# Degrees and scaling of a graph layer: zeros in quarters, a short reciprocal, low parts on VectorE

## The chip, the cores and the metric

The kernel runs on 1 core of one Trainium2 chip. Its time is device microseconds of one execution; the figure for a kernel is the median of its runs.

## The reference

1250 nodes with 512 features each, 21,250 weighted edges (1250 of them loops), ten propagation steps, then an LSTM over the 1250 rows in which each step picks one of four weight sets:

```python
def _L0_gnn_ref(x, alpha, beta, sigma, edge_val, edge_row, edge_col, num_iters):
    xn = x * rsqrt(maximum(sum(x * x, axis=1, keepdims=True), 1e-12))
    sim_e = sum(xn[edge_row] * xn[edge_col], axis=-1)
    sim_e = where(edge_row == edge_col, 0.0, sim_e)
    sim_e = exp(sim_e / (2.0 * sigma_sq))            # sigma_sq = 2 exp(sigma)^2
    sup = edge_val * sim_e
    normalize = segment_sum(sup, edge_row, num_segments=n)
    denom = b + normalize[:, None] * a + a           # a = exp(alpha), b = exp(beta)
    def step(out, _):
        Ax = segment_sum(sup[:, None] * out[edge_col], edge_row, num_segments=n)
        return (x * b + (Ax + out) * a) / denom, None
    out, _ = scan(step, x, None, length=10)

x = x + _L0_gnn_ref(_layernorm(x), alpha, beta, sigma, edge_weight, src, dst, 10)
x = x + _L0_ffn_ref(_layernorm(x)[None], ...)[0]     # the LSTM with a choice of weight set per step
```

## The kernel before

The graph is worked as a dense matrix. The 1250 nodes are padded to NP = 1280, ten row blocks (RT) of 128 partitions. The steps follow each other in this order.

**Head.** VectorE (from line 619) zeroes the last block of X, then all 12,801 columns of the SBUF tile Adj1 (line 620), then sets `ones` and `ident` and zeroes the three edge tiles; the last of these (`ew`, line 625) releases six edge loads on ScalarE's DMA queue (lines 492 to 495), which already carries five small loads. SyncE's queue loads X (lines 286, 287) and then, released by the zeros, writes Adj1 into each of two adjacency tensors in DRAM (lines 289 to 291, 51,204 bytes to a partition). TensorE spreads the scalars over the partitions when `ones` and the five small loads are there (line 908), VectorE copies them out (631), ScalarE, whose program has the six edge issues first, forms exp(alpha), exp(beta) and exp(-2 sigma) (498, 499), and VectorE scales the last (633). Only behind this wait does VectorE do the layernorm and the normalization (661 to 670). TensorE transposes the result, ScalarE takes it out of PSUM (513).

**Scatter.** 42 rounds of four edge columns: VectorE writes the keys on a diagonal (691), TensorE spreads them over the partitions by a product with `ones` (941), VectorE compares (694, 695), TensorE sums the weights of edges with equal keys (944), and GpSimd scatters them into the DRAM tensors by an indirect DMA (371 to 379, profile line 375) with a wait for an earlier one to have landed. The first scatter waits for the zeros (366). Between the rounds TensorE computes the similarities and ScalarE their exponentials into Adj.

**Adjacency.** SyncE's queue reads the two tensors back, row block by row block (293 to 300). VectorE adds them in Adj1 (720) and multiplies the sum into Adj (723).

**Degrees.** When all ten blocks are done, TensorE sums Adj over its rows, column piece by column piece (512, 512, 256), all row blocks of a piece one after the other; because the left operand is `ones`, each degree stands in every partition (951 to 955). An f32 matmul has two records in the profile. VectorE then forms 1/(a deg + b + a) for all 1280 columns in every partition (726 to 729) into inv_b, takes its diagonal blocks as per-partition columns `den` (730 to 732), and scales (733 to 735).

**Scaling and splitting.** For each row block, VectorE multiplies Adj by inv_b (738) and adds the diagonal (740); ScalarE rounds the block to f16, the high part (526); GpSimd subtracts it from the f32 value, which gives the f16 low part (411, 412). Both go into M_parts, which lies over Adj1. VectorE waits for all ten low parts (743), writes T (745) over Adj, and ScalarE and GpSimd split T in the same manner (530, 416).

**Propagation** (lines 750 to 755, 957 to 971) is ten times 300 f16 matmuls of 128x512. **After it** come the residual, a second layernorm, the projections of the first 64 rows and the splitting of the recurrent weights. **Recurrence** (lines 829 to 886, 1000 to 1082): each of the 1250 steps computes the gates with a guessed weight set and, where the guess was wrong, again with the chosen one (`repeated`). Fifteen semaphores are raised by one by VectorE ahead of it (824 to 826); the first logit product waits for `c_ready`, the fourteenth of them.

The order is set by each engine's program order and the semaphores. Where `link` stands, VectorE waits for its own instruction's end before the next.

Of the kernel before, what the change touches and what calls it, by code (L numbers as in the profile page):

```python
# [5 lines left out]
def gnn_then_selected_lstm(  # L6
# [40 lines left out]
    ITERS = 10  # L47
    COLS = [(c, min(512, NP - c)) for c in range(0, NP, 512)]
# [21 lines left out]
    with ctx:  # L70
# [66 lines left out]
        inv_b = sim[:, 0, :]  # L137

# [76 lines left out]
        deg_mm = sem("deg_mm")  # L215
        prop_mm = sem("prop_mm")
# [66 lines left out]
        def _(sp):  # L283
# [6 lines left out]
            for b in range(2):  # L290
                sp.dma_start(adj[b].rearrange("(p n) -> p n", p=P), Adj1[:, :]).then_inc(adj_zeroed, 16)
# [61 lines left out]
        def _(pool):  # L353
# [9 lines left out]

            last_word = pool.alloc_register("last_word")
            pool.reg_mov(last_word, P * CW - 1)
            pool.wait_ge(adj_zeroed, 32)
# [42 lines left out]

            for r in range(RT):  # L410
                pool.wait_ge(m_high, r + 1)
                pool.tensor_tensor(M_parts[:, 1, r, :], Adj[:, r, :], M_parts[:, 0, r, :], ALU.subtract).then_inc(m_low, 1)
# [198 lines left out]
        def _(dve):  # L611
# [8 lines left out]
            dve.memset(Adj1[:, :], 0.0).then_inc(zero_set, 1)  # L620
# [4 lines left out]
            dve.memset(ew[:, :], 0.0).then_inc(edge_ready, 1)  # L625
            for s in range(S):
                link(dve.memset(ramp[:, s:s + 1], float(S - s)))
# [97 lines left out]
            dve.wait_ge(deg_mm, 1)  # L725
            for c, (c0, m) in enumerate(COLS):
                link(dve.tensor_scalar(inv_b[:, c0:c0 + m], ps[:, c, 0:m], ab[:, 0:1], ab[:, 1:2], ALU.mult, ALU.add))
            link(dve.tensor_scalar(inv_b, inv_b, ab[:, 0:1], None, ALU.add))
            link(dve.reciprocal(inv_b, inv_b))
            for r in range(RT):  # L730
                link(dve.scalar_tensor_tensor(out=junk[:, 0, :], in0=inv_b[:, r * P:(r + 1) * P], scalar=1.0, in1=ident[:, :],
                                              op0=ALU.mult, op1=ALU.mult, accum_out=den[:, r:r + 1]))
            link(dve.tensor_scalar(adn[:, :], den[:, :], ab[:, 0:1], float(2 ** MS), ALU.mult, ALU.mult))
            link(dve.tensor_scalar(bdn[:, :], den[:, :], ab[:, 1:2], float(2 ** OS), ALU.mult, ALU.mult))
# [169 lines left out]
        def _(pe):  # L904
# [47 lines left out]
            for c, (c0, m) in enumerate(COLS):  # L952
                for r in range(RT):
                    last = nc.tensor.matmul(ps[:, c, 0:m], ones[:, :], Adj[:, r, c0:c0 + m], start=(r == 0), stop=(r == RT - 1))
# [192 lines left out]
```

## Time and profile before

| | |
|---|---|
| median of 3 runs | 6814.86 us (6814.09 to 6822.49) |
| profiled execution, its own time | 6817.24 us |
| its span, first to last instruction | 6815.5 us |
| mean granted TensorE clock | 0.959 |
| busy: PE matmul, VectorE, ScalarE, GpSimd | 6117.3, 3616.7, 1805.4, 1686.4 us |
| DMA moved | 389.94 MB |

All times below are microseconds from the span's start unless marked ns. PE is TensorE's matmul, PEld its weight load, DVE VectorE, ACT ScalarE, POOL GpSimd, SP SyncE; ACTq and SPq are their DMA queues. A timeline row has its start, its duration, the engine, the line, the operation, output and inputs by name and shape, xN where N such instructions are merged, and in brackets how long the engine was idle before it and what ended that. Tiles that lie over one another appear under one name: Adj in a row can be Adj1, T or M_parts, and sim can be inv_b. A source-line row has the count, minimum, median and maximum duration in ns and the first and last start. On the page a group has busy time and mean ns of one, then the idle time before it and its releaser. The clock is the share of full speed that was granted.

### The profile page before, as it was taken

Reading aid. Unit: us, or ns where it says so; the run is one execution under the profiler, and the core shown is the slowest. Engines: PE = TensorE matmul, PEld = TensorE weight load, DVE = VectorE, ACT = ScalarE, POOL = GpSimd, SP = SyncE. Lnnn points to the kernel's source line nnn. Section 1 sums busy time; section 2 is a strip of 40 time slices with the busy share of each in tenths; the row PEclk is TensorE's granted clock in tenths of the full one; section 3 lists DMA queues with packets and bytes.
Section 4 is the critical chain, followed back from the end, with each engine's and each line's share of the span. In section 5 each row is a group of like instructions: output and inputs, shape, how many; then the busy total and the mean of one; then the engine's idle time right before and its main releaser. Section 6 shows DMA issues by size and latency. Waiting matters only on the chain.

```text
span 6815.5 us, 340711 instructions
## 1 busy us (share of the span) xinstructions
PE 6117.3 (90%) x126674; PEld 4119.5 (60%) x126675; DVE 3616.7 (53%) x19152; ACT 1805.4 (26%) x6561; POOL 1686.4 (25%) x4128
## 2 busy tenths in 40 slices
PE   6727999789999999999999999999999999999986
PEld 3523444666666666666666666666666666666663
DVE  5553111245565556555665555566556655556555
ACT  1001000522332223223332333233333333233321
POOL 4733111412222222222222222222222222222220
PEclk8758999589999999999999999999999999999999
DMA  3230000622222122122222222222222222222210
GB/s 95 1 77 0 0 0 0 192 71 58 62 63 58 57 60 65 55 60 60 65 63 60 62 61 60 60 63 63 61 60 65 64 61 63 59 63 62 61 52 27
DMA packets 691011, 389.94 MB, mean 57 GB/s; under 512 B 47835, under 2 KB 670811, under 8 KB 690720
## 3 DMA queue, kind: packets, MB, share of 16 engines
q1 hardware_dynamic: 659746, 369.66, 18.5%
q0 software_dynamic: 24192, 0.10, 1.1%
q10 hardware_dynamic: 7038, 19.69, 0.9%
q8 instruction: 26, 0.43, 0.0%
q14 instruction: 9, 0.07, 0.0%
HBM read 370.96 MB, written 18.38 MB: 57 GB/s over the span
## 4 chain that ended last, share of the span: by engine, by line
PE 70%; DVE 6%; issue 5%; DMA 1%; DVEq 0%; SPq 0%; ACT 0%; POOL 0%; POOLq 0%
PE ps L1016 33%; PE ps L1078 15%; PE ps L1025 8%; PE ps L1009 5%; PE ps L1005 4%; DVE hsum L843 2%; PE ps L1002 2%; PE ps L991 1%; DVE osum L851 1%; DVE acts L861 1%; DVE gates L848 1%; DVE osum L854 1%; DMA wring<-in_w_ih 1%; DVE cprod L857 0%; PE ps L978 0%
## 5 line engine op out<-in xcount | busy, mean ns | idle before, releaser
L1016 PE MATMUL ps<-WH,hparts 128*2 128x384 f16 x49760 | 2303.0, 326 | 196.6 <-issue 176.1
L1016 PEld LDWEIGHTS ps<-WH,hparts 128*2 128x2 f16 x49760 | 1053.4, 83 | 1044.7 <-issue 292.9
L843 DVE TRANSPOSE_TENSOR_REDUCE hsum<-ps 128x12 f32<-128x384 f32 x1250 | 728.7, 583 | 1793.0 <-PE ps L1016 1788.0
L1078 PE MATMUL ps<-xcur,wcur 128*128 128x64 f32 x9728 | 1341.9, 281 | 85.7 <-issue 12.4
L1078 PEld LDWEIGHTS ps<-xcur,wcur 128*128 128x128 f32 x9728 | 1178.5, 191 | 273.3 <-issue 210.2
L454 POOL COPY xT<-hfull 128x4 f32 x1250 | 239.5, 192 | 3727.2 <-DVE hfull L872 3727.2
L470 POOL COPY wcur<-wring 128x512 f32<-128x512 f32 x1216 | 743.4, 611 | 445.1 <-ACT gxb L598 443.3
L1025 PEld LDWEIGHTS ps<-WH,hparts 128*2 128x2 f16 x40000 | 603.7, 83 | 352.7 <-issue 314.9
L1025 PE MATMUL ps<-WH,hparts 128*2 128x128 f16 x40000 | 781.2, 219 | 7.5
L583 ACT ACTIVATE gx_now<-gxb 128x16 f32 x1250 | 269.7, 216 | 1782.2 <-DVE pick L837 1707.1
L969 PE MATMUL ps<-O,Adj 128*128 128x512 f16 x3000 | 650.3, 380 | 77.2 <-DVEq L748 77.2
L598 ACT ACTIVATE gxb<-ps,ubias,gscale 128x64 f32 x1216 | 562.2, 462 | 327.4 <-PE ps L1078 247.5
L586 ACT ACTIVATE acts<-gates 128x12 f32<-128x12 f32 x1250 | 265.4, 212 | 1378.1 <-DVE gates L848 1378.1
L969 PEld LDWEIGHTS ps<-O,Adj 128*128 128x128 f16 x3000 | 294.1, 98 | 433.3 <-issue 81.1
L1005 PE MATMUL ps<-wselT,acts 128*1 128x4 f32 x10000 | 433.4, 166 | 20.4 <-DVE acts L861 4.2
L1009 PE MATMUL ps<-owsel,tanc 128*1 128x4 f32 x10000 | 428.1, 166 | 0.0
L851 DVE TRANSPOSE_TENSOR_REDUCE osum<-ps 128x4 f32<-128x128 f32 x1250 | 385.4, 308 | 0.1
L754 DVE SCALAR_TENSOR_TENSOR Adj<-ps,Adj 128x512 f32<-128x512 f32 x100 | 69.2, 692 | 582.2 <-PE ps L969 582.2
L1005 PEld LDWEIGHTS ps<-wselT,acts 128*1 128x1 f32 x10000 | 317.6, 81 | 54.2 <-DVE acts L861 48.1
L1009 PEld LDWEIGHTS ps<-owsel,tanc 128*1 128x1 f32 x10000 | 326.8, 81 | 31.2
L588 ACT ACTIVATE otan<-osum 128x4 f32<-128x4 f32 x1250 | 256.6, 205 | 263.8 <-DVE osum L854 263.8
L375 POOL DMA_INDIRECT adjacency<-total,where_ x168 | 261.4, 1556 | 129.4 <-issue 79.4
(147 smaller groups left out, 4983.8 us busy)
## 6 DMA issues: line engine op xcount, KB each, us to landing
wring<-in_w_ih SPq DMA_DIRECT2D x1280, 256.0 KB, 2.9
gxb<-in_w_hh ACTq DMA_DIRECT2D x32, 512.0 KB, 5.6
adjacency<-Adj SPq DMA_DIRECT2D x2, 6400.5 KB, 24.7
Adj<-adjacency SPq DMA_DIRECT2D x10, 640.0 KB, 7.5
sim<-adjacency SPq DMA_DIRECT2D x10, 640.0 KB, 6.3
adjacency<-total,where_ POOLq DMA_INDIRECT x168
x_rows<-X SPq DMA_DIRECT2D x1, 2560.0 KB, 8.7
wring<-x_rows SPq DMA_DIRECT2D x10, 256.0 KB, 3.5
```

Of the source, the lines that this page charges most:

```text
L470: pool.tensor_copy(wcur[:, :, :], wring[:, u, :, :]).then_inc(wcur_set, 1)
L583: act.activation(gx_now[:, :], gxb[:, bass.ds(t % (2 * TB), 1), bass.ds(r * (G * SUB) - G * SUB, G * SUB)].rearrange("p t c -> p (t c)"), ...
L586: act.activation(acts[:, 0:3 * SUB], gates[:, :], ACT.Tanh, scale=1.0 / GATE_SCALE).then_inc(acts_ready, 1)
L598: act.activation(gxb[:, bass.ds(((b + 1) % 2) * TB, TB), bass.ds(i, 1)].rearrange("p t c -> p (t c)"), unit_ps, ACT.Identity, scale=gscale ...
L843: dve.tensor_reduce(hsum[:, :], gate_ps.rearrange("p (c q) -> p c q", q=32), AX.X, ALU.add, apply_transpose=True).then_inc(turned, 1)
L851: dve.tensor_reduce(osum[:, 0, :], ogate_ps.rearrange("p (c q) -> p c q", q=32), AX.X, ALU.add, apply_transpose=True).then_inc(oturned, 1)
L969: last = nc.tensor.matmul(ps[:, r % 8, :], M_parts[:, m_part, c, r * P:(r + 1) * P], old[:, o_part, c, :], start=(c == 0 and m_part + o_pa ...
L1005: nc.tensor.matmul(logit_ps, acts[:, 3 * SUB + k:3 * SUB + k + 1], wselT[:, k, :], start=False, stop=False)
L1009: last = nc.tensor.matmul(logit_ps, tanc[:, k:k + 1], owsel[:, k, :], start=False, stop=(k == SUB - 1))
L1016: last = nc.tensor.matmul(gate_ps[32 * j:32 * j + 2, :], hparts[:, k, :], WH[:, s * KC + k, part, j, 0:3 * P], start=(k == 0 and part == 0 ...
L1025: last = nc.tensor.matmul(ogate_ps[32 * j:32 * j + 2, :], hparts[:, k, :], WH[:, s * KC + k, part, j, 3 * P:4 * P], start=(k == 0 and part ...
L1078: last = nc.tensor.matmul(unit_ps, wcur[:, k, :], xcur[:, k, :], start=(k == 0), stop=(k == KC - 1))
```

## The change

The zeros: Adj1's first quarter (ZC = 3201 columns) alone is zeroed, after the memset of the edge weights, and each adjacency tensor is zeroed by four DMAs from it. The degrees: the loops change places, so that TensorE sums a row block as soon as it is masked, into three PSUM banks. The reciprocal: VectorE takes the ten per-partition degrees from the diagonals of the sums, forms the reciprocal of these 10 columns alone, writes a (1/den) 2^15 on ten diagonal 128x128 tiles, TensorE spreads each over the partitions by a product with `ones`, and VectorE copies the result to inv_b in three pieces. The low parts of the matrix go from GpSimd to VectorE, each behind the next block's product. Five of the fifteen counts ahead of the recurrence are raised by GpSimd before its first scatter.

```diff
--- before.py
+++ after.py
@@ -45,6 +45,8 @@
     NN = NP * NP
     CW = NN // P + 1
     ITERS = 10
+    ZC = -(-CW // 4)
+    ZEROS = [(z, min(ZC, CW - z)) for z in range(0, CW, ZC)]
     COLS = [(c, min(512, NP - c)) for c in range(0, NP, 512)]
     TB = 64
     BLOCKS = -(-N // TB)
@@ -135,6 +137,7 @@
         XB = adj_words[:, 0:RT * D].rearrange("p (t d) -> p t d", t=RT)
         T = adj_words[:, RT * D:2 * RT * D].rearrange("p (t d) -> p t d", t=RT)
         inv_b = sim[:, 0, :]
+        adiag = [one[:, q, :] for one, part in ((kdiag, range(NQ)), (same, range(NQ)), (junk, range(2, NQ))) for q in part]
 
 
         WH = sb("WH", [P, S * KC, 2, 4, D], f16)
@@ -213,6 +216,8 @@
         sim_exp = sem("sim_exp")
         adj_ready = sem("adj_ready")
         deg_mm = sem("deg_mm")
+        adiag_set = sem("adiag_set")
+        arow_mm = sem("arow_mm")
         prop_mm = sem("prop_mm")
         m_ready = sem("m_ready")
         m_high = sem("m_high")
@@ -288,7 +293,8 @@
 
             sp.wait_ge(zero_set, 2)
             for b in range(2):
-                sp.dma_start(adj[b].rearrange("(p n) -> p n", p=P), Adj1[:, :]).then_inc(adj_zeroed, 16)
+                for z0, zn in ZEROS:
+                    sp.dma_start(adj[b].rearrange("(p n) -> p n", p=P)[:, z0:z0 + zn], Adj1[:, 0:zn]).then_inc(adj_zeroed, 16)
 
             for b in range(2):
                 sp.wait_ge(scattered[b], 16 * EIT * (NQ // 2))
@@ -361,9 +367,13 @@
                                pattern=[[-1, P]], channel_multiplier=1).then_inc(masks, 1)
             pool.iota(dump_i[:, :], pattern=[[0, 1]], base=NN, channel_multiplier=1).then_inc(masks, 1)
 
+
+            for one in (guess_mm, settled, ogate_mm, gx_set, acts_ready):
+                pool.sem_inc(one, 1)
+
             last_word = pool.alloc_register("last_word")
             pool.reg_mov(last_word, P * CW - 1)
-            pool.wait_ge(adj_zeroed, 32)
+            pool.wait_ge(adj_zeroed, 16 * 2 * len(ZEROS))
             for q in range(NQ):
                 pool.sem_inc(places_free[q], 1)
 
@@ -407,10 +417,6 @@
                 landed(2, second)
             landed(3, 32 * EIT)
 
-            for r in range(RT):
-                pool.wait_ge(m_high, r + 1)
-                pool.tensor_tensor(M_parts[:, 1, r, :], Adj[:, r, :], M_parts[:, 0, r, :], ALU.subtract).then_inc(m_low, 1)
-
             def low_part(new, r, n):
                 pool.wait_ge(t_high, n)
                 pool.tensor_tensor(new[:, 1, r, :], T[:, r, :], new[:, 0, r, :], ALU.subtract).then_inc(t_low, 1)
@@ -617,12 +623,12 @@
                 dve.wait_ge(v, chain[0])
 
             dve.memset(X[:, RT - 1, :], 0.0).then_inc(zero_set, 1)
-            dve.memset(Adj1[:, :], 0.0).then_inc(zero_set, 1)
             dve.memset(ones[:, :], 1.0).then_inc(consts, 1)
             dve.memset(ident[:, :], 0.0).then_inc(consts, 1)
             dve.memset(src_i[:, :], 0)
             dve.memset(dst_i[:, :], 0)
             dve.memset(ew[:, :], 0.0).then_inc(edge_ready, 1)
+            dve.memset(Adj1[:, 0:ZC], 0.0).then_inc(zero_set, 1)
             for s in range(S):
                 link(dve.memset(ramp[:, s:s + 1], float(S - s)))
 
@@ -723,22 +729,32 @@
                 dve.tensor_tensor(Adj[:, r, :], Adj[:, r, :], Adj1[:, r * NP:(r + 1) * NP], ALU.mult).then_inc(adj_ready, 1)
 
             dve.wait_ge(deg_mm, 1)
+            for r in range(RT):
+                link(dve.scalar_tensor_tensor(out=junk[:, 0, :], in0=ps[:, r // 4, (r % 4) * P:(r % 4 + 1) * P], scalar=1.0, in1=ident[:, :],
+                                              op0=ALU.mult, op1=ALU.mult, accum_out=den[:, r:r + 1]))
+            link(dve.tensor_scalar(den[:, :], den[:, :], ab[:, 0:1], ab[:, 1:2], ALU.mult, ALU.add))
+            link(dve.tensor_scalar(den[:, :], den[:, :], ab[:, 0:1], None, ALU.add))
+            link(dve.reciprocal(den[:, :], den[:, :]))
+            link(dve.tensor_scalar(adn[:, :], den[:, :], ab[:, 0:1], float(2 ** MS), ALU.mult, ALU.mult))
+            for r in range(RT):
+                dve.tensor_scalar(adiag[r], ident[:, :], adn[:, r:r + 1], None, ALU.mult).then_inc(adiag_set, 1)
+            link(dve.tensor_scalar(bdn[:, :], den[:, :], ab[:, 1:2], float(2 ** OS), ALU.mult, ALU.mult))
+            dve.wait_ge(arow_mm, RT)
             for c, (c0, m) in enumerate(COLS):
-                link(dve.tensor_scalar(inv_b[:, c0:c0 + m], ps[:, c, 0:m], ab[:, 0:1], ab[:, 1:2], ALU.mult, ALU.add))
-            link(dve.tensor_scalar(inv_b, inv_b, ab[:, 0:1], None, ALU.add))
-            link(dve.reciprocal(inv_b, inv_b))
-            for r in range(RT):
-                link(dve.scalar_tensor_tensor(out=junk[:, 0, :], in0=inv_b[:, r * P:(r + 1) * P], scalar=1.0, in1=ident[:, :],
-                                              op0=ALU.mult, op1=ALU.mult, accum_out=den[:, r:r + 1]))
-            link(dve.tensor_scalar(adn[:, :], den[:, :], ab[:, 0:1], float(2 ** MS), ALU.mult, ALU.mult))
-            link(dve.tensor_scalar(bdn[:, :], den[:, :], ab[:, 1:2], float(2 ** OS), ALU.mult, ALU.mult))
-            link(dve.tensor_scalar(inv_b, inv_b, ab[:, 0:1], float(2 ** MS), ALU.mult, ALU.mult))
+                link(dve.tensor_copy(inv_b[:, c0:c0 + m], ps[:, 4 + c, 0:m]))
+
+            def low_of_m(r):
+                dve.wait_ge(m_high, r + 1)
+                dve.tensor_tensor(M_parts[:, 1, r, :], Adj[:, r, :], M_parts[:, 0, r, :], ALU.subtract).then_inc(m_low, 1)
 
             for r in range(RT):
                 link(dve.tensor_tensor(Adj[:, r, :], Adj[:, r, :], inv_b, ALU.mult))
                 blk = Adj[:, r, r * P:(r + 1) * P]
                 dve.scalar_tensor_tensor(out=blk, in0=ident[:, :], scalar=adn[:, r:r + 1], in1=blk,
                                          op0=ALU.mult, op1=ALU.add).then_inc(m_ready, 1)
+                if r > 0:
+                    low_of_m(r - 1)
+            low_of_m(RT - 1)
 
             dve.wait_ge(m_low, RT)
             for r in range(RT):
@@ -821,7 +837,7 @@
             dve.memset(hparts[:, :, :], 0.0).then_inc(h_ready, 1)
 
 
-            for one in (guess_mm, settled, ogate_mm, turned, gx_set, oturned, acts_ready, cprod_ready, otan_ready, osig_ready,
+            for one in (turned, oturned, cprod_ready, otan_ready, osig_ready,
                         tanc_ready, h_high, owsel_ready, c_ready, unit_out):
                 dve.sem_inc(one, 1)
             dve.sem_inc(hist_free, 2)
@@ -948,11 +964,15 @@
             for q in range(NQ):
                 pe.wait_ge(edge_out[q], EIT)
 
-            pe.wait_ge(adj_ready, RT)
-            for c, (c0, m) in enumerate(COLS):
-                for r in range(RT):
+            for r in range(RT):
+                pe.wait_ge(adj_ready, r + 1)
+                for c, (c0, m) in enumerate(COLS):
                     last = nc.tensor.matmul(ps[:, c, 0:m], ones[:, :], Adj[:, r, c0:c0 + m], start=(r == 0), stop=(r == RT - 1))
             last.then_inc(deg_mm, 1)
+
+            for r in range(RT):
+                pe.wait_ge(adiag_set, r + 1)
+                nc.tensor.matmul(ps[:, 4 + r // 4, (r % 4) * P:(r % 4 + 1) * P], ones[:, :], adiag[r], start=True, stop=True).then_inc(arow_mm, 1)
 
             pe.wait_ge(prop_ready, 1)
             with pe.Fori(0, ITERS // 2) as i:
```

## Rows read from the trace of the kernel before

**Rows 1.** Timeline from the start to the first scatter
```profile
4.10 10.73 DVE L620 MEMSET Adj<- 128x12801 f32 x1 [2.62 <-issue]
...
15.46 0.20 DVE L625 MEMSET ew<- 128x168 f32 x1
...
20.46 1.14 ACTq L495 DMA_DIRECT2D ew<-in_ew_tail  x1
...
23.25 0.15 DVE L633 TENSOR_SCALAR ab<-ab 128x1 f32<-128x1 f32 x1 [7.00 <-ACT ab L499]
...
61.18 1.72 POOL L375 DMA_INDIRECT adjacency<-total,where_  x1 [45.26 <-DVE total L708]
```

**Rows 2.** GB/s in 40 slices of 60 us; landings of the adjacency
```profile
GB/s 0 57 190 330 391 374 365 60 0 0 546 546 0 546 553 553 519 34 553 553 560 0 553 546 552 518 40 553 519 553 35 80 0 0 0 0 0 0 0 0
...
DMA to landing us min/median/max: 4.9/6.6/32.7
```

**Rows 3.** Windows: length; busy PE, PEld, DVE, ACT, POOL; clock, DMA, GB/s
```profile
456.50:480.20 23.70, 23.60 (x60) 12.09 (x60) 0.00 (x0) 0.00 (x0) 0.00 (x0) 0.92 0.00 1
480.20:496.40 16.20, 0.00 (x0) 0.00 (x0) 15.54 (x28) 0.00 (x0) 0.00 (x0) 0.63 0.00 0
496.40:539.50 43.10, 0.00 (x0) 0.00 (x0) 38.74 (x20) 12.70 (x10) 26.06 (x10) 0.50 0.00 0
```

**Rows 4.** Masked product of each row block; weight loads of the degree matmuls
```profile
L723 DVE TENSOR_TENSOR Adj<-Adj x10: 1491/1491/1493, 422.4 to 455.0; 128x1280 f32<-128x1280 f32 x10
...
460.14 0.32 PEld L954 LDWEIGHTS ps<-Adj,ones 128*128 128x128 f32 x1 [0.52 <-issue]
...
464.13 0.19 PEld L954 LDWEIGHTS ps<-Adj,ones 128*128 128x128 f32 x1 [0.24 <-issue]
```

**Rows 5.** Timeline of VectorE after the degree matmuls
```profile
480.24 2.24 DVE L727 TENSOR_SCALAR sim<-ps,ab 128x512 f32<-128x512 f32 x3 [23.79 <-PE ps L954]
...
483.43 8.15 DVE L729 RECIPROCAL sim<-sim 128x1280 f32<-128x1280 f32 x1
...
491.62 0.29 DVE L731 SCALAR_TENSOR_TENSOR junk<-sim,ident 128x128 f32<-128x128 f32 x1
...
494.95 0.23 DVE L733 TENSOR_SCALAR adn<-den,ab 128x10 f32<-128x10 f32 x1
```

**Rows 6.** Timeline of the nearest rows for the new operations
```profile
30.70 0.22 DVE L642 RECIPROCAL rstd<-root 128x10 f32<-128x10 f32 x1 [0.34 <-ACT root L503]
...
52.72 0.87 DVE L691 TENSOR_SCALAR kdiag<-ident,key 128x128 f32<-128x128 f32 x4 [0.26 <-DVE to_dump L684]
...
56.86 1.16 PE L941 MATMUL ps<-kdiag,ones 128*128 128x128 f32 x8 [0.91 <-ACT xT L513]
...
57.65 0.34 DVE L695 SCALAR_TENSOR_TENSOR junk<-ps,key,below 128x128 f32<-128x128 f32 x1
```

**Rows 7.** Timeline of the row blocks of the scaled adjacency
```profile
497.93 0.35 DVE L740 SCALAR_TENSOR_TENSOR Adj<-ident,adn,Adj 128x128 f32<-128x128 f32 x1
...
499.67 2.61 POOL L412 TENSOR_TENSOR Adj<-Adj 128x1280 f16<-128x1280 f32 x1 [93.05 <-ACT Adj L526]
499.72 2.71 DVE L740 SCALAR_TENSOR_TENSOR Adj<-ident,adn,Adj 128x128 f32<-128x128 f32 x1
...
502.46 1.27 ACT L526 ACTIVATE Adj<-Adj 128x1280 f16<-128x1280 f32 x1 [2.87 <-DVE Adj L740]
```

**Rows 8.** Timeline around the start of the recurrence
```profile
1392.79 0.06 DVE L821 MEMSET hparts<- 128x4 uint32 x1
...
1394.06 0.34 PE L1005 MATMUL ps<-wselT,acts 128*1 128x4 f32 x8 [1.28 <-DVEq L826]
```

**Rows 9.** Page: instruction queue and recurrence matmuls; chain: an early issue wait
```profile
q8 instruction: 26, 0.43, 0.0%
...
L1016 PE MATMUL ps<-WH,hparts 128*2 128x384 f16 x49760 | 2303.0, 326 | 196.6 <-issue 176.1
...
1398.03 2.65 issue
```

## Prediction, made before the changed kernel was run

> **What bounds the kernel now.** I read the windows by stage first: they show one chain of stages with hardly any overlap between them. The zeroed tensors, layernorm and transposes run to the first scatter at 61.2 us; scatters, which GpSimd paces, and their landing to 413.9; then the adjacency is read and masked, its degrees are formed, it is scaled and split, and ten propagation steps and the recurrence follow. The recurrence is some 5,420 of the 6,815.5 us and the change leaves its body alone, so all that can be won lies in the 560 us ahead of the propagation, and what is won there moves everything behind it forward by as much.
>
> Second, the timeline up to the first scatter [rows 1]. VectorE fills all 12,801 columns with zeros (10.73 us) ahead of the memsets that release the edge loads. ScalarE's queue issues those six loads until 21.6 us, only then forms the exponentials, and VectorE stands for 7.00 us until 23.25. The landing row shows the cover there is: the second zero transfer was issued at about 15.3 us and took 32.7, so the tensors are zero at 48 us, 13 us before GpSimd's first scatter, which waited for VectorE [rows 1, 2].
>
> Third, the degree and scaling stages. TensorE works 23.6 of 23.7 us on the degrees while every other engine is idle; then VectorE alone works 15.5 of 16.2 us; then VectorE is busy 38.7 of 43.1 us, GpSimd 26.1 [rows 3]. In the last of these the timeline shows why: the diagonal addition takes 0.35 us alone and 2.71 us where it starts 0.05 us behind a GpSimd low part of 2.61 us [rows 7].
>
> **The sum.** It is made against the profiled execution, 6817.24 us with a span of 6815.5; the median of the three runs, 6814.86, lies 2.4 us under it.
>
> **Zeros and head.** With the long memset behind the memset of the edge weights, these end 10.7 us earlier, at about 4.95 us, if the idle 2.62 us ahead of the second memset stay. The quarter memset costs 10.73/4 = 2.7 us and ends at 7.7 us, beside ScalarE's issues. These end at 21.6 - 10.7 = 10.9, and VectorE's wait ends at about 12.6. Every later step up to the first scatter is VectorE's own work, TensorE's and ScalarE's, and shifts whole: 50.6 instead of 61.2. Three covers are needed. X must be in by 12.6: its transfer is seen in the slices until about 12 us [rows 2], and I take it as just enough. The small tensors that the exponentials need travel beside X and are in with it at the latest; if they came only at 12, VectorE would start at about 14.6, and the gain would be 8.6. If neither the 2.62 us nor that wait were there, X's 12 us would bind and the gain be 11.5. The zeros must be in by 50.6: eight issues at about 0.43 us each, 7.7 to 11.2 us, queue behind X, and 13.1 MB take 32 us as now, which gives 44; at the 375 GB/s of X's transfer they take 35 us and end at 47. The slack of 13 us shrinks to 3 to 7. I take **10.6**, ends 8.6 and 11.5. GpSimd's five early counts cost nothing: it idles 45 us there. The scatters (two queues and GpSimd, untouched) take as long as before.
>
> **Degrees.** Ten masked row blocks end between 423.9 and 456.5 us, one every 3.6 us [rows 4]. One block is a tenth of the degree matmuls. At the low clock a weight load comes every 0.84 us, later every 0.43 [rows 4]; twenty 512-wide and ten 256-wide matmuls are two loads each, so a block costs about 2.1 us at 2.4 GHz and 4.2 at 1.2. At the low clock TensorE would be saturated by rows 3.6 us apart and would then rise as it does now within 4 us; afterwards it has gaps of 1.5 us and may fall again. So the tail behind the last row is 2.1 (high all the time) to 5.4 us (low, one block behind). I take 3.4 in place of the 23.8 between 456.45 and 480.24: **20.4**, ends 18.4 and 21.7. TensorE's waits hold nothing but these matmuls behind them, and its reads hinder no transfer that I see.
>
> **Reciprocal chain.** Before: 480.24 to 496.40, 16.2 us, 8.15 of them the 1280-wide reciprocal [rows 5]. After: ten diagonal sums from PSUM. From SBUF they come every 0.33 us; the nearest PSUM row takes 0.34 instead of 0.29 [rows 5, 6], so 0.385 each, 3.85 us. Three 10-wide operations at 0.27 and a short reciprocal at 0.25 are 1.06. The first diagonal tile follows after 0.3; VectorE makes one every 0.22, but each feeds a matmul: four took 1.16 us, 0.29 each [rows 6], and at the low clock, with 128 columns where a 512-wide one takes two loads' 1.7, about 0.43. TensorE's clock is at its low level for most of 480 to 496 (mean 0.63) [rows 3], after some 4 us of idleness, and here it idles 5, so I take the low one: 4.6 with its end. VectorE waits for the tenth and, behind that wait, copies three column pieces (1.9 us, against 2.24 for the scaling of rows 5). Together 11.7 us. Ends: 9.7 with the fast matmuls, 14 if each matmul also waits out its own release. **4.5**, ends 2.2 and 6.5. The saved long reciprocal is thus half given back to a broadcast through TensorE.
>
> **Row blocks.** Before 43.1 us, 4.1 a block, of which 2.6 is GpSimd. After, VectorE does all: product 1.51, diagonal 0.28 (0.35 with its overlap, as in the first block, since GpSimd is idle), low part of the block before. That last one is in no row for VectorE. Its nearest is the two-input product of the same width, 1.49 us [rows 4]; above, GpSimd's own 2.61; below, half of 1.49 plus overhead, 0.9. I take 1.51: 3.30 a block, 33.0 us. The Trainium skill (VectorE: DVE Perf Modes, What auto-detection actually checks) allows an operation with two sources only one faster mode, and only if every tensor is 16-bit; here two of three are not wholly so (f32 in, f16 out), so it speaks for 1.5 and against 0.9; by the other value the sum would gain 6 us more. ScalarE's 1.27 us high part lies under the next product and diagonal (1.79), with 0.4 to spare; after the last block it is bare for nothing, since the ninth low part (1.5) covers it. **10.1**, ends -1 and 16. GpSimd's later low parts are untouched, and it comes to them earlier than they are asked for.
>
> **Counts.** 1.2 us lie between the end of the last memset and TensorE's first logit product, behind 14 counts [rows 8]: 0.086 each, five fewer, **0.4**.
>
> Sum: 10.6 + 20.4 + 4.5 + 10.1 + 0.4 = 46.0. From 6817.2 that is 6771.2, from the median 6768.9; I say **6770**.
>
> **Rivals.** *The head is not won.* Zeros in pieces or X beside the edge loads come late, so that the first scatter stays near 61 us: 6770 + 10.6 = 6781. For it: the slack is 3 to 7 us, and both queues now start together. Against: the bytes are the same and start 7 us earlier. 8%.
> *The low part is as dear on VectorE as on GpSimd*, 2.6 us: 11 more, 6781. Against: the 1.49 us row of equal width. 4%.
> *The degrees are not overlapped*, the change not doing what it says, because the three sums held open together or the waits per row keep TensorE behind: 20.4 lost, 6790. Against: the loop waits for one row at a time, and the three sums lie in three banks. 2%.
> *Slower: the recurrence pays for moved code.* TensorE's program grows ahead of a loop with eight branch targets. The page shows 26 instruction transfers in all, and its chain a wait of 2.65 us in one of the first steps, where a branch goes to a new place [rows 9]. 49,760/32 - 1250 = 305 steps are repeated after a wrong guess. If each paid such a wait: 305 x 2.65 = 808 us, 7578. It decides from 60 us on, 0.2 us per repeated step. Against: 26 transfers cannot serve 1250 steps, so the loop stays in place now. The Trainium skill (Runtime: NRT & Kernel Launch, Instruction fetch mechanics) says that a taken branch whose target isn't in the current window forces a fetch before execution can continue; no run here shows where that window's edge lies against this loop. 2%.
>
> **The numbers.** Forecast 84%. Its own ends, taken half together, are 6758 and 6780; the first two rivals lie at 6781, so 6758 to 6783 leaves out the last two and some tails. A measurement of this kernel tells 0.2%, 13.6 us, from no change. Faster 0.97: all cases but the last. Same 0.01, for several of them at once. Slower 0.02.
>
> **What would show it.** First scatter near 50.6; VectorE's scaled sigma (line 633 now) at 12.6, and no wait for X behind it; degree matmuls between the row products, VectorE's first diagonal sum about 3.4 us after the last product; first product of the scaling 11.7 us later; diagonal additions of 0.35 throughout and low parts of 1.5 on VectorE; span 46 us shorter with the stretch from the scaling's end to the end unchanged but for 0.4. A zero transfer or X as releaser of a wait, low parts over 2 us, or repeated steps longer than before would make it wrong.

## The result: 1.1% faster, more than the whole range forecast

The changed kernel took 6742.2 us (median of 4 runs, 6730.7 to 6751.0) beside 6815.6 before; the ratio is 0.9887, 95% interval 0.9874 to 0.9900. A second measurement of the same kernel, beside its own runs of before, gave 0.9889 (0.9874 to 0.9904). So the gain is 73 to 79 us where 46 were forecast, and the time lies 16 us under the range of 6758 to 6783. The profiled execution took 6730.7 us with a span of 6728.9. It was the fastest of the four, so the table by stages below adds up to 86.6 us between the two profiles, not to 73.

From the page of the changed kernel; line 1036 is line 1016 of before [rows 9]:

```profile
span 6728.9 us, 340768 instructions
...
q8 instruction: 24, 0.39, 0.0%
...
L1036 PE MATMUL ps<-WH,hparts 128*2 128x384 f16 x49760 | 2291.6, 326 | 181.9 <-issue 161.0
```

TensorE's matmuls of the recurrence are as many and as long, but "issue" time ahead of them is 15 us less than in [rows 9], in a part whose code and data the change doesn't touch. That is the first sign of where the unforeseen gain lies.

The head, in the changed kernel's timeline (it answers to [rows 1]):

```profile
2.11 0.20 DVE L630 MEMSET ew<- 128x168 f32 x1
2.92 2.73 DVE L631 MEMSET Adj<- 128x3201 f32 x1 [0.62 <-issue]
...
5.68 3.95 SPq L297 DMA_DIRECT2D adjacency<-Adj  x8
5.81 0.32 ACTq L501 DMA_DIRECT2D ew<-in_ew_tail  x1
...
9.91 0.56 PE L924 MATMUL ps<-scal,ones 1*128 1x7 f32 x2 [9.91 <-DMA wsel<-in_w_sel_state]
...
11.11 0.15 DVE L639 TENSOR_SCALAR ab<-ab 128x1 f32<-128x1 f32 x1 [0.36 <-ACT ab L505]
13.14 6.03 DVE L656 BATCH_NORM_STATS2 stats<-X 128x6 f32<-128x512 f32 x10 [1.88 <-DMA X<-in_x]
```

The edge issues end at 6.1 us, not 10.9: the idle 2.62 us ahead of the second memset are gone, and five of the six issues took 0.33 instead of 1.1. Two other things came in their place, both named in the prediction as covers and both underrated: TensorE's product waited for the last small load until 9.91, and VectorE then waited 1.88 us for X. The layernorm starts at 13.14 instead of 23.32, the first scatter comes at 50.66 instead of 61.18, and no zero transfer is late.

The degrees and the reciprocal, in its timeline (for [rows 4, 5]):

```profile
413.40 1.19 PEld L970 LDWEIGHTS ps<-Adj,ones 128*128 128x128 f32 x3 [0.52 <-issue]
...
418.04 0.19 PEld L970 LDWEIGHTS ps<-Adj,ones 128*128 128x128 f32 x1 [0.24 <-issue]
...
441.00 2.42 PE L970 MATMUL ps<-Adj,ones 128*128 128x512 f32 x6 [0.70 <-DVE Adj L729]
...
443.46 0.29 DVE L733 SCALAR_TENSOR_TENSOR junk<-ps,ident 128x128 f32<-128x128 f32 x1 [2.51 <-PE ps L970]
...
446.80 0.29 DVE L735 TENSOR_SCALAR den<-den,ab 128x10 f32<-128x10 f32 x1
...
447.91 0.87 DVE L740 TENSOR_SCALAR kdiag<-ident,adn 128x128 f32<-128x128 f32 x4
448.25 1.78 PEld L975 LDWEIGHTS ps<-kdiag,ones 128*128 128x128 f32 x8 [5.23 <-DVE kdiag L740]
...
452.99 1.87 DVE L744 COPY sim<-ps 128x512 f32<-128x512 f32 x3 [2.90 <-PE ps L975]
454.90 1.49 DVE L751 TENSOR_TENSOR Adj<-Adj,sim 128x1280 f32<-128x1280 f32 x1
```

The first block and half of the second are summed at the low clock (a weight load every 0.85 us), the rest at the high one (every 0.43), and it stays high through TensorE's gaps of 0.4 to 1.7 us. Behind the last masked row stand six matmul records, 2.4 us. Then VectorE sums a diagonal every 0.333 us, from PSUM as fast as from SBUF, and the ten broadcasts begin at 448.25 and the copies at 452.99, 4.7 us later.

The windows of these stages (in the column behind the five engines, the granted clock: 0.50 is the low level, 1.00 the high one), of the row blocks, and of the recurrence, from the first reduction of the gates to the end (columns as in [rows 3]):

```profile
409.80:413.40 3.60, 3.55 (x5) 1.50 (x5) 2.98 (x2) 0.00 (x0) 0.00 (x0) 0.50 1.00 361
...
417.50:443.40 25.90, 19.30 (x48) 8.47 (x48) 20.89 (x14) 0.00 (x0) 0.00 (x0) 1.00 0.73 282
...
440.90:443.50 2.60, 2.42 (x6) 1.06 (x6) 0.09 (x2) 0.00 (x0) 0.00 (x0) 1.00 0.00 0
443.50:454.90 11.40, 4.64 (x20) 4.34 (x20) 7.91 (x38) 0.00 (x0) 0.00 (x0) 0.70 0.00 0
...
448.20:452.90 4.70, 4.64 (x20) 4.34 (x20) 1.90 (x10) 0.00 (x0) 0.00 (x0) 0.51 0.00 0
...
454.90:486.90 32.00, 0.00 (x0) 0.00 (x0) 31.64 (x30) 12.70 (x10) 0.00 (x0) 0.52 0.00 0
...
1339.50:6728.90 5389.40, 5040.50 (x121975) 3473.15 (x121963) 3174.55 (x17537) 1609.85 (x6215) 1184.37 (x3732) 1.00 0.21 60
```

For the same stretch of the recurrence in the kernel before:

```profile
1397.20:6815.50 5418.30, 5052.57 (x121978) 3499.71 (x121967) 3173.47 (x17537) 1610.32 (x6215) 1191.32 (x3732) 1.00 0.21 60
```

The row blocks take 32.0 instead of 43.1 us [rows 3], with VectorE busy 31.6 and GpSimd not at all. The recurrence takes 5389.4 instead of 5418.3 us. Inside a block (for [rows 7]) the diagonal addition takes 0.35 us each time and the low part 1.49, the next product starting 1.40 behind it:

```profile
461.40 0.35 DVE L753 SCALAR_TENSOR_TENSOR Adj<-ident,adn,Adj 128x128 f32<-128x128 f32 x1
461.67 1.49 DVE L748 TENSOR_TENSOR Adj<-Adj 128x1280 f16<-128x1280 f32 x1
461.79 1.27 ACT L532 ACTIVATE Adj<-Adj 128x1280 f16<-128x1280 f32 x1 [1.92 <-DVE Adj L753]
463.07 1.49 DVE L751 TENSOR_TENSOR Adj<-Adj,sim 128x1280 f32<-128x1280 f32 x1
```

All stages together, both profiled executions, from their starts in the timelines:

| stretch, ended by | before | after | less | forecast |
|---|---|---|---|---|
| head, first scatter | 61.2 | 50.7 | 10.5 | 10.6 |
| scatters and landing, first read of the adjacency | 352.7 | 349.6 | 3.1 | 0 |
| read and mask, last product | 42.5 | 40.7 | 1.8 | 0 |
| degrees and reciprocal, first scaled row | 40.0 | 13.9 | 26.0 | 24.9 |
| row blocks, T | 43.1 | 32.1 | 11.1 | 10.1 |
| T, propagation | 669.0 | 669.3 | -0.3 | 0 |
| up to the first gates | 188.8 | 183.3 | 5.5 | 0.4 |
| first 20 steps | 100.4 | 94.3 | 6.1 | 0 |
| next 1160 steps | 4975.6 | 4955.9 | 19.7 | 0 |
| last steps and output | 342.2 | 339.3 | 2.9 | 0 |

The last row was 338.2 to 342.2 us in all fifteen profiles but the two with VectorE's stop (348 and 351), so its 2.9 us are not put down to anything.

### The profile page after: what moved, and what is told of

It reads as the page before. It is cut to its first block, busy times and chain, and to the rows that moved or that the text cites. A ratio compares the mean times of both kernels' runs of the same rounds, so it can differ in the third digit from the quotient of the medians.

```text
span 6728.9 us, 340768 instructions
## 1 busy us (share of the span) xinstructions
PE 6107.5 (91%) x126694; PEld 4091.9 (61%) x126695; DVE 3595.2 (53%) x19172; ACT 1804.8 (27%) x6561; POOL 1652.7 (25%) x4118
## 4 chain that ended last, share of the span: by engine, by line
PE 70%; DVE 6%; issue 5%; DMA 1%; DVEq 0%; ACT 0%; SPq 0%; POOL 0%; POOLq 0%
PE ps L1036 34%; PE ps L1098 16%; PE ps L1045 8%; PE ps L1029 5%; PE ps L1025 4%; DVE hsum L859 2%; PE ps L1022 2%; PE ps L1011 1%; DVE osum L867 1%; DVE acts L877 1%; DVE gates L864 1%; DVE osum L870 1%; DMA wring<-in_w_ih 1%; DVE cprod L873 0%; PE ps L998 0%
## 5 line engine op out<-in xcount | busy, mean ns | idle before, releaser
L1036 PEld LDWEIGHTS ps<-WH,hparts 128*2 128x2 f16 x49760 | 1037.7, 83 | 1044.2 <-issue 282.2
L1045 PEld LDWEIGHTS ps<-WH,hparts 128*2 128x2 f16 x40000 | 595.3, 83 | 350.7 <-issue 308.6
L1025 PE MATMUL ps<-wselT,acts 128*1 128x4 f32 x10000 | 428.3, 166 | 20.4 <-DVE acts L877 4.1
```

What stands on the lines that cost most here:

```text
L1025: nc.tensor.matmul(logit_ps, acts[:, 3 * SUB + k:3 * SUB + k + 1], wselT[:, k, :], start=False, stop=False)
L1036: last = nc.tensor.matmul(gate_ps[32 * j:32 * j + 2, :], hparts[:, k, :], WH[:, s * KC + k, part, j, 0:3 * P], start=(k == 0 and part == 0 ...
L1045: last = nc.tensor.matmul(ogate_ps[32 * j:32 * j + 2, :], hparts[:, k, :], WH[:, s * KC + k, part, j, 3 * P:4 * P], start=(k == 0 and part ...
```

## The experiments

Each kernel is the one before, or the changed one, with the edit shown. Beside the time I read the middle of the recurrence, the 1160 steps from the 21st reduction of the gates to the 1181st (4975.6 us before). The theory was that this middle depends on where an engine's loop lies in its program, which the change moves: its place, counted in instructions from the program's start. The rival was that it is drawn anew in each execution. A stop, in what follows, is a gap in which an engine has work and waits for nothing that the trace shows; a set is one of the four weight sets; and a repeated step is one of the 305 whose guess was wrong, so that TensorE branches to the gate products of the chosen set.

**The changed kernel again.** No edit.

> The changed kernel, unaltered. In the first profiled executions the stretch from the first to the last transposing reduction of the gates (the recurrence) took 5389.5 us before and 5361.7 after, and the four runs of the changed kernel spread over 20 us. Theory P (the recurrence is shorter because TensorE's program has 59 more instructions ahead of it, so its branches lie elsewhere): the stretch is again 5362 within 3 us, and the runs spread little. Theory L (the length of the recurrence is drawn anew in each execution and has nothing to do with the change): the stretch lies anywhere between 5360 and 5390.

0.9889 of before; middle 4956.5, where the first profile had 4955.9. So it is fixed by the kernel. What did differ between the two executions lay ahead: the scatters took 337.6 instead of 341.3 us, and the stretch from the propagation up to the projections 3 us less. Over all fifteen profiles that leave these stages alone or move them whole, the scatters took 337.4 to 343.9, the reading and masking 40.7 to 44.4, in no order that follows the edits. The 5 us of these rows of the table are therefore spread between executions, not the change. So are most of the 5.5 us in the row up to the first gates: from the last propagation product to the first projection it took 65.4 us before and 60.8 after, and 58.6 to 65.4 over the fifteen.

**Instructions in TensorE's program, the rest as before.** `pads` is a semaphore that nobody waits for; its declaration is left out here.

```diff
+            for _ in range(59):
+                pe.sem_inc(pads, 1)
             pe.wait_ge(adj_ready, RT)
```

> The kernel before with 59 increments of an unused semaphore in TensorE's program, in its idle time ahead of the degree matmuls, as many instructions as the change adds there. Theory P: the recurrence falls from 5389.5 to about 5362 us and the kernel is some 25 us faster (about 6790), with everything ahead of the recurrence as before. Theory L: nothing moves by more than the spread of the runs, 6814 to 6822.

0.9959 (0.9945 to 0.9972), 30 us by the medians, without any work taken away; middle 4957.0. The two profiles are 35 us apart: 23.7 of them lie between the first and the last reduction of the gates (5365.8 us instead of 5389.5), most of the rest in the scatters (337.4 for 343.9). The place theory holds, the rival falls. (The change itself adds 40 instructions to TensorE's program by the built program, not 59; that the middle is the same with 40 and 58 shows that the exact number isn't what counts.)

**The zeros alone.** The edit is that of the change.

> The kernel before with the zeros alone changed. Sum of the prediction: 10.6 us at the first scatter (50.6 instead of 61.2). The first profile after the change showed 10.5 there and 3 us more up to the adjacency's first read; theory P and L both expect these 3 us to be the scatter loop's own spread (a gain of 8 to 14 in all), a third theory (Z: the first scatters gain from the earlier end of the zero transfers) expects 13 to 14. The recurrence stays at 5389.5 under P; under L it may be anywhere in 5360 to 5390. Time about 6804.

0.9987 (0.9977 to 0.9996), 10.2 us by the medians; the first scatter came at 51.6 us, the middle took 4982.8. Nothing shows that the zero transfers give anything beyond the head: the scatters and their landing took 348.3 us, inside the spread of the other runs.

**The counts alone.** The edit is that of the change.

> The kernel before with the five counts alone moved to GpSimd. Sum of the prediction: 0.4 us, seen between the last memset of the state and the first logit product (1.27 us before, 0.8 after). If the moved counts (and VectorE's shorter program) are what shortens the recurrence, it falls towards 5362 us and the time to about 6790; under P it stays at 5389.5 and the time at 6815.

1.0000 (0.9991 to 1.0009). In this profile the first logit product came 3.35 us behind the memset, not 0.8; the 0.5 us that the whole change shows there in all four of its profiles drown in such differences here. Middle 4983.1.

**The degrees alone.**

```diff
-            pe.wait_ge(adj_ready, RT)
-            for c, (c0, m) in enumerate(COLS):
-                for r in range(RT):
+            for r in range(RT):
+                pe.wait_ge(adj_ready, r + 1)
+                for c, (c0, m) in enumerate(COLS):
```

> The kernel before with the degree loops changed alone (9 more waits in TensorE's program). Stage: the prediction's tail behind the last masked row is 3.4 us (2.1 to 5.4) instead of 23.8; the first profile after the change showed 2.5. So VectorE starts the scaled degrees 20 to 21.5 us earlier. Recurrence: under the place theory it is some number between 5362 and 5397 that 9 more instructions decide, with the same 160 ns stops behind some branch targets moved or gone; under the theory that only 59 or more help, it is as before (5390 to 5397).

0.9969 (0.9959 to 0.9979), 21 us; last masked row to first scaled row 18.7 instead of 40.0 us. The middle, 4977.7, is as before. My count was wrong: in the built program a wait rides on the matmul behind it, so TensorE's program has no instruction more.

**The short reciprocal alone.** The edit is that of the change, with the degree loops as before.

> The kernel before with the short reciprocal and its broadcast through TensorE alone (50 more instructions in TensorE's program). Stage: the prediction has 11.7 us (9.7 to 14) from the end of the degree sums to the first scaled row block instead of 16.2; the first profile after showed 11.4. Recurrence as for the run of the degrees: place theory, anything in 5362 to 5397 decided by 50 instructions.

0.9956 (0.9939 to 0.9972), 30 us: 4.8 in its stage (35.2 instead of 40.0), 20.8 in the middle (4954.8) and 5.6 in the first 20 steps. Its ten f32 matmuls are 40 instructions of TensorE's program, and these, not their work, bring most of the gain.

**The low parts alone.** The edit is that of the change.

> The kernel before with the low parts of the matrix on VectorE alone, TensorE's program untouched. Stage: 33.0 us predicted (32.05 in the first profile after) instead of 43.1. Recurrence: the place theory for TensorE's program expects what the other kernels with its program unchanged have, 5389 to 5397; so the gain in all is 10 to 11 us, against before with its own 5389.5 perhaps 4 less.

1.0150 (1.0133 to 1.0166), 100 us slower, though the row blocks take 32.05 us, where 33.0 were forecast. The middle is 5081.2: 106 us more in 1160 steps. VectorE's rows show where. Before, between the product for the next logits and the one that forms h:

```profile
3002.44 0.17 DVE L867 SCALAR_TENSOR_TENSOR owsel<-otan,wselT 128x16 f32<-128x16 f32 x1
...
3002.64 0.16 DVE L872 TENSOR_TENSOR hfull<-osig,tanc 128x4 f32<-128x4 f32 x1
```

With the low parts alone:

```profile
3004.74 0.17 DVE L870 SCALAR_TENSOR_TENSOR owsel<-otan,wselT 128x16 f32<-128x16 f32 x1
...
3005.04 0.16 DVE L875 TENSOR_TENSOR hfull<-osig,tanc 128x4 f32<-128x4 f32 x1
```

0.30 instead of 0.20 us, in every step of the loop, on the path to the next gates. VectorE's program is 10 instructions longer ahead of the loop. The instruction queues carry nothing in the middle of this trace, as in that of before: both pages have 26 transfers on q8, and none of q8 or q14 lies in these 1160 steps.

**VectorE's program longer by 10, the rest as before.**

```diff
+            for _ in range(10):
+                dve.sem_inc(pads, 1)
             dve.wait_ge(deg_mm, 1)
```

> The kernel before with 10 increments of an unused semaphore in VectorE's program, in its idle time ahead of the degrees, so that its recurrence loop lies where it lies in the kernel with the low parts alone (the product that forms h is instruction 452 instead of 442 of VectorE's program). No other engine's program changes. Place theory for VectorE: a stop of 103 ns ahead of that product in each of the 1250 steps, the middle of the recurrence 5081 instead of 4976 us, the time some 6815 + 100 = 6915. If the low parts themselves (VectorE's or GpSimd's work, the missing GpSimd instructions) cause the 104 us, the time stays at 6815.

1.0164 (1.0147 to 1.0181), 113 us slower; middle 5085.9; and the same rows:

```profile
3000.16 0.17 DVE L870 SCALAR_TENSOR_TENSOR owsel<-otan,wselT 128x16 f32<-128x16 f32 x1
...
3000.46 0.16 DVE L875 TENSOR_TENSOR hfull<-osig,tanc 128x4 f32<-128x4 f32 x1
```

**The low parts with one VectorE instruction more.** The same edit with `range(1)`, on the kernel with the low parts alone.

> The kernel with the low parts alone plus one such increment in VectorE's program (h's product is instruction 453, as in the kernel with the short reciprocal alone, which showed no stop). Place theory: the stop of 103 ns moves ahead of an instruction that waits anyway, the middle of the recurrence returns from 5081 to 4976 to 4983 and the time from 6918 to 6803 to 6808, so that the 11 us of the row blocks show. Otherwise it stays at 6918.

0.9982 (0.9972 to 0.9992), 6805.4 us; middle 4983.0. One instruction moved, and 112 us are gone. Instruction 452 of the built program is now not h's product but a wait ahead of it, so I take the stop to lie inside that wait; it shows nowhere:

```profile
3002.19 0.17 DVE L873 SCALAR_TENSOR_TENSOR owsel<-otan,wselT 128x16 f32<-128x16 f32 x1
...
3002.39 0.16 DVE L878 TENSOR_TENSOR hfull<-osig,tanc 128x4 f32<-128x4 f32 x1
```

One of its ten executions took 18744 us; no run here says why.

**TensorE's program longer still.** The edit of 59 with 5 on the changed kernel, and with 129 and 257 on the one before.

> The changed kernel with 5 increments more in TensorE's program, which makes 64 more instructions than before. If the stops of 160 ns behind branch targets depend on where the target lies within a block of 64 or fewer instructions (a power of two), the targets are back where they were: the repeated sets 1 and 3 stop again, the recurrence goes from 5362 back to about 5390 and the time from 6734 to some 6755 to 6760. If only the distance from the program's start or a larger block counts, the time stays at 6734.

6743.4 us, 0.9893 (0.9877 to 0.9910), middle 4955.8: no stop came back. The run doesn't test what its expectation says, for by the built program the kernel is 44 instructions longer than before, not 64.

> The kernel before with 128 instructions more in TensorE's program. Before, 160 ns stops stand behind the entries of the repeated sets 1 and 3, whose places (4709 and 4450) lie 259 apart with the stops 256 apart, so I suppose one edge every 256 instructions. Moved by 128, the edges come 3 to 4 behind the entry of set 2 and at the entry of set 0: sets 1 and 3 lose their stops, set 2 gets one (about 75 repeated steps x 0.1 to 0.16 us = 8 to 12 us), set 0 may. Middle of the recurrence 4955 + 8 to 25 = 4963 to 4980. If the stops came at smaller steps (128 or fewer), sets 1 and 3 keep them.

0.9979 (0.9969 to 0.9989), middle 4974.2. The repeated sets 1 and 3 lost their stops and set 2 got one: its 83 repeated steps took 1764 ns in the median (1594 to 1862) from their first gate weight load to the reduction, 1593 before (1592 to 1594). Set 0 got none.

> The kernel before with 256 instructions more in TensorE's program. If an edge lies every 256 instructions, everything is back where it was: the stops behind the entries of the repeated sets 1 and 3 are there as before, the middle of the recurrence is 4976 to 4983 us and the time as before, 6815. If the total length or a larger block decides, the sets 1 and 3 run without stops as with 40, 45 and 58 instructions more, 4955 and 6785.

1.0001 (0.9991 to 1.0011), middle 4978.3, with the stops behind the entries of sets 1 and 3 where they were. So what makes a stop, an edge in TensorE's program, comes again after 256 instructions, and 128 are not enough. I sorted the repeated steps of the middle by the set they branch to; this is the mean time of such a step in us, from one reduction to the next, with those that stop in bold:

| branch to | steps | before | + 59 | + 129 | + 257 | changed | changed + 217 |
|---|---|---|---|---|---|---|---|
| set 0 | 74 | 5.96 | 5.96 | 5.97 | 5.96 | 5.96 | 5.96 |
| set 1 | 60 | **6.01** | 5.84 | 5.85 | **6.01** | 5.83 | **6.00** |
| set 2 | 79 | 5.85 | 5.85 | **6.02** | 5.86 | 5.85 | 5.85 |
| set 3 | 65 | **5.81** | 5.71 | 5.72 | **5.81** | 5.71 | **5.81** |

**The changed kernel at the old place.** The edit with 217 on the changed kernel.

> The changed kernel with 216 instructions more in TensorE's program, so that its recurrence lies 256 instructions behind its place in the kernel before, where the run with 256 more had its stops back. Place theory: the repeated sets 1 and 3 stop again, the middle of the recurrence is 4976 to 4983 instead of 4956 us, the time is 20 to 27 us above the changed kernel's 6734 to 6742, about 6760, and its gain over the kernel before is what the change's own work is worth, 50 to 57 us. If the changed kernel's gain in the recurrence came from its own work, the time stays at 6734 to 6742.

6769.1 us, 0.9927 (0.9913 to 0.9940), 52.6 us under before by the medians; middle 4978.6, first 20 steps 100.7 instead of 94.3. In it the stages ahead of the recurrence are those of the changed kernel (13.4 us from the last masked row to the first scaled one, 13.9 in its own profile). Only TensorE's program is put back; VectorE's stays 16 instructions further on, where it shows no stop (h's product 1758 ns after the reduction, 1757 before). One and the same step of all four, the 235th, whose guess is wrong, from one reduction of the gates to the next. Before, 6.01 us:

```profile
2435.52 0.58 DVE L843 TRANSPOSE_TENSOR_REDUCE hsum<-ps 128x12 f32<-128x384 f32 x1 [0.95 <-PE ps L1016]
...
2441.53 0.58 DVE L843 TRANSPOSE_TENSOR_REDUCE hsum<-ps 128x12 f32<-128x384 f32 x1 [3.06 <-PE ps L1016]
```

Before with 256 more, 6.02:

```profile
2432.29 0.58 DVE L844 TRANSPOSE_TENSOR_REDUCE hsum<-ps 128x12 f32<-128x384 f32 x1 [0.95 <-PE ps L1019]
...
2438.31 0.58 DVE L844 TRANSPOSE_TENSOR_REDUCE hsum<-ps 128x12 f32<-128x384 f32 x1 [3.06 <-PE ps L1019]
```

Changed with 216 more, 6.01:

```profile
2384.05 0.58 DVE L860 TRANSPOSE_TENSOR_REDUCE hsum<-ps 128x12 f32<-128x384 f32 x1 [0.95 <-PE ps L1039]
...
2390.06 0.58 DVE L860 TRANSPOSE_TENSOR_REDUCE hsum<-ps 128x12 f32<-128x384 f32 x1 [3.06 <-PE ps L1039]
```

Changed, 5.85:

```profile
2368.04 0.58 DVE L859 TRANSPOSE_TENSOR_REDUCE hsum<-ps 128x12 f32<-128x384 f32 x1 [0.95 <-PE ps L1036]
...
2373.89 0.58 DVE L859 TRANSPOSE_TENSOR_REDUCE hsum<-ps 128x12 f32<-128x384 f32 x1 [2.94 <-PE ps L1036]
```

| kernel | TensorE's loop moved by | VectorE's h product is instruction | middle, us |
|---|---|---|---|
| before; degrees; zeros | 0 | 442 | 4975.6; 4977.7; 4982.8 |
| counts | 0 | 437 | 4983.1 |
| before + 59 | 58 | 442 | 4957.0 |
| before + 129 | 128 | 442 | 4974.2 |
| before + 257 | 256 | 442 | 4978.3 |
| low parts; VectorE + 10 | 0 | 452 | 5081.2; 5085.9 |
| low parts + 1 | 0 | 453 | 4983.0 |
| reciprocal | 40 | 453 | 4954.8 |
| changed; again | 40 | 458 | 4955.9; 4956.5 |
| changed + 5 | 44 | 458 | 4955.8 |
| changed + 217 | 256 | 458 | 4978.6 |

## Why the prediction was wrong

**The change's own work was forecast well.** Put back at the old place, the changed kernel gains 52.6 us by the medians, 41 to 59 by the ratio's interval; the sum was 46.0. The terms, as the stages of the profiles show them, come to 48.1:
- Head 10.6: 10.5, by a balance of two errors. The 2.62 us of idleness went and the issues ran faster, but the small loads (9.91) and X (13.14) took their place; X, which I took as just enough, was 0.5 us late.
- Degrees 20.4: the tail is 2.5 us, not 3.4, for the clock rose in the second block and stayed up. 21.3.
- Reciprocal chain 4.5: 16.2 became 11.4; the diagonal sums were cheaper (0.333 for 0.385), the broadcasts ran at the low clock as assumed (0.46 us each for 0.43). 4.7.
- Row blocks 10.1: 3.19 us a block, not 3.30, because a low part passes on after 1.40. 11.1. The Trainium skill's rule (VectorE: DVE Perf Modes, What auto-detection actually checks) agrees with the 1.49 us of the row: no faster mode with f32 in. (Of the low part's three tensors one is f32, the minuend; the prediction's "two of three" is wrong, and one is enough.)
- Counts 0.4: 0.47 in the profile.

The range was wider than it says. Its lower end, 6758, is what all four favourable ends give at once (11.5 + 21.7 + 6.5 + 16 + 0.4 under 6814.9 is 6758.8), not half of them. So no size of these terms within its ends reaches 6742: something outside the sum was missing.

**The step that failed** is the sentence that "the change leaves its body alone, so all that can be won lies in the 560 us ahead of the propagation". The recurrence is 1250 passes through code whose place every earlier instruction shifts. The rival had the mechanism, moved code, but with one sign: I asked what new stops the move could bring and took the present place as free of any. It wasn't. Of the repeated steps in the middle of the trace of before, the 60 into set 1 lose 0.17 us each behind the entry and the 65 into set 3 lose 0.10 each in the products, against the kernel with 59 more; that is 10.3 and 6.6 of the 18.6 us between the middles of these two (against the changed kernel, 17.4 of 19.7).

Another 6 us lie in the first 20 steps, which took 98 to 101 us in the kernels at the old place (and 102 with VectorE's stop) and 94.1 to 95.4 in the others that were moved. These are of another kind, for nearly all of it stands in the first three steps (25.6 us before, 19.7 after), and there instructions are transferred. From the profile's DMA queues over the first 20 steps, before:

```profile
q8 instruction: 5, 0.08, 0.3%
```

and changed:

```profile
q8 instruction: 3, 0.05, 0.3%
```

All nine profiles at the old place have 5 on q8 there and 22.7 to 25.8 us for three steps; the six that were moved have 2 or 3, and 19.4 to 20.9 us. In the 1160 steps of the middle none of the fifteen traces has a transfer on q8, and one of them, that of the counts, has a single one on q14. So the prediction's premise that "26 transfers cannot serve 1250 steps" was right, and its conclusion that the loop therefore runs without such costs was not: the stops come without a transfer.

The rival's price was off as well: 2.65 us was that of a first visit, a stop in place costs 0.10 to 0.17 on TensorE and 0.10 on VectorE. The signs were in reach: 176 us of "issue" ahead of the gate products [rows 9] were read as a number to compare with and not asked what they are.

**The sum of both.** The own work's 52.6 and the place's some 26 (6769.1 against 6742.2 and 6743.4, or 35 against the 6733.9 of the second measurement) are the gain measured, 73 to 79 us. Of the 26 to 35, traces show 22.7 in the middle and 6.4 in the first 20 steps.

**Open.** The middle of kernels at the same place differs by 7 us (4975.6 for before, 4982.8 with the zeros), and no run tells why; in the second, every repeated step takes some 10 ns more from the load of the chosen set to the first repeated weight load (996 for 986 at set 0), and every other step 3 ns more in the median. Of the 19.7 us in the middle, 2 are spread over the steps that are not repeated. What makes the stops isn't shown. Shown are their place, their size and, on TensorE, their period of 256 instructions; that no instruction transfer goes with them speaks against a fetch from memory in each, and leaves open what the engine does at an edge.

## What to carry to other kernels

A loop that runs a thousand times is part of every change made ahead of it: its branch entries lie somewhere against edges 256 instructions apart, and an edit that adds ten instructions can cost or give more than the work it saves. Measure a change at the old place too, by padding the engine's program until its loop has moved by a multiple of 256 instructions (shown here for TensorE; for VectorE only places within 21 instructions were measured), before its gain or loss is put down to what it does; the low parts alone would have been given up as 1.5% slower, and with one instruction more were 0.2% faster (12.7 us), as their stage says (11). And when a rival about a resource has a price, ask for it with both signs: what it would cost if it came, and what it costs already.

## What the runs showed that I had not expected

- VectorE's loop across an edge: 103 ns in every step of the loop where the instruction behind the edge is on the path (h's product at 1861 instead of 1758 ns after the reduction), nothing where a wait stands there. The Trainium skill (Runtime: NRT & Kernel Launch, Instruction fetch mechanics) has engines load instructions in blocks of 256 and calls the cost of crossing a boundary mostly hidden. The period agrees with the 256 that TensorE's runs show; the cost does not: where it is exposed it makes 1.6% of this kernel, on VectorE, where the period itself was not tested.
- TensorE pays 0.10 to 0.17 us where an edge lies within some four instructions behind a taken branch's target (4709 and 4450 in its program before, and set 2's with 128 more), and nothing that shows where it lies in the middle of a straight run of products (set 2's, with 58 more: 5.85 us, as before).
- The clock stayed at its high level while TensorE worked 2.4 of every 3.1 to 4.1 us on the row blocks (granted 1.00 from 417.5 to 443.4), and was low again for the broadcasts after 4.8 us without work (0.51).
